# Attention of six heads on one Trainium2 core: products with V in four column groups instead of three, in twelve lots per image instead of sixteen

## Chip, cores and metric

The kernel runs on one core of one Trainium2 chip. The metric is the device time of one execution in microseconds. PE is TensorE, DVE is VectorE, ACT is ScalarE, POOL is GpSimd, SP is the engine that issues the DMAs.

## What is computed

The input is 32 images of 192 channels and 32 x 32 pixels, that is 1024 tokens of 192 numbers. Each image goes through three parts, each with a residual sum:

```python
x = x + proj(channel_attention(x))                  # 8 heads over channels, l2-normed
t = tokens(x)                                       # [B, 1024, 192]
z = ln(t); q, k, v = z @ Wq, z @ Wk, z @ Wv         # 6 heads of 32
att = softmax(causal(q @ k.T / sqrt(192)))
t = t + att @ v                                     # the part that is changed
t = t + ffn(ln(t))                                  # sign weights, absmax over groups of images
```

The causal attention is the large part: for each of 6 heads and each of 8 query tiles of 128 tokens, a query tile qt (0 to 7) sees the key tiles 0 to qt, so qt + 1 tiles.

## The kernel before, in words

**Groups and images.** 32 images are worked in five groups of six and a rest of two (`groups`, L343). A group is one long `attention` (PE L659, ACT L914, DVE L1202) over its six images, and then a tail (`group_tail`) with the feed-forward part of the six.

**Units and slots.** A unit is one head and one query tile; an image has UNITS = 48 of them (L48). The order of all the work is written out by hand in slots, one slot per unit, and each engine goes through the same slots in the same order. In slot n:

- PE makes the scores of unit n in PSUM (`S`, L672), adds the causal mask (L674), and turns (transposes) the probabilities of unit n - 3 (AHEAD, L53) into one or two banks `PT` of up to four tiles each (L686);
- DVE takes the row maximum of the scores of unit n (L1206) and copies the first bank of unit n - 3 from PT to SBUF (L378, called from `pt_copy`);
- ACT makes exp of unit n (L929) and copies the second bank of unit n - 3, if its qt is over 3 (L933, `by_act`).

The two halves of `S` alternate, so PE's scores of unit n + 2 wait for exp of unit n. The two banks PT alternate too, so a turn waits until the bank before last was copied. Small units (qt 0 to 3) are the even ones and large units (qt 4 to 7) the odd ones (TILES, L52).

**Products with V.** P times V needs the turned probabilities as the moving operand, 128 columns of f32, and 32 columns of V (one head) as weights. A lot of them (before: a triple, `triple_of`, L72) takes three units of the same query tile and of heads 3*grp to 3*grp + 2. Head number hh of a triple goes to PE's column group 32*hh and to rows 32*hh of the PSUM bank `OUT`, with `tile_position=(0, 32*hh)` (L706 to L708). The loop is over key tiles j outside and heads inside; I call one j of a lot a step. A triple of query tile qt has qt + 1 steps, each of three products, each of which is two matmul instructions. Triples run at slots 8 (small) and 11 (large) after the start of their block of six slots (PV_AT, L54), after the turns of that slot. An image has KI = 16 triples.

**Going back.** Four triples (BATCH, L55) fill the four places of 128 columns in `OUT`. ACT copies OUT to `oT` (L921, at slot OT_AT), PE turns oT into a PT bank (L715, at BACK_AT), and DVE (`add_to_t1`) multiplies by the reciprocals of the row sums and adds to `T1` (L1192, L1194, L1200). NBI = 4 such batches per image.

**Buffers of turned probabilities.** `PTS` is in `work`: a ring of four places for small units (4 x 512 columns) and of four for large ones (4 x 1024). `pt_copy` waits until the triple that last read the place has been multiplied (`pv_made`).

**Front work.** Beside the attention of image u, the channel attention, the layer norm and the projections of image u + 1 run in slots that SLOTS (L153) and SMALL_SLOTS (L158) fix: xt0 to xt3, g0, g1, wg0, wg1, na, rb, u, mt, t0 to t3, then z0 to z3, qk0 to qk5 and v0 to v3. On the way from "rb" (slot 15) to "u" (slot 18) lie the small channel softmax on DVE (logits, slot 16, L1109 to L1116), ACT (xexp, slot 17, L857) and DVE (attn, slot 17.5, L1119 and L1122). Layer norm statistics and normalisation are on DVE at slots 22, 25, 27, 28 and 29. After qk5, SP sends q and k with 16 DMAs per image to QS and KS (`front` of SP, L412 to L417), eight for heads 0 to 2 and then eight for heads 3 to 5; PE waits for the second eight at slot 24 (L663 to L665), and DVE at slot 9 (wg0, L1092). The slots of the front work are not touched by the change.

Of the kernel before, what the change touches and what calls it, by code (L numbers as in the profile page):

```python
# [18 lines left out]
F32 = mybir.dt.float32  # L19
# [40 lines left out]
RING = 4  # L60
STACKS = 8 * 16
# [5 lines left out]

def qtile(n):
    return TILES[n // 6 % 4][n % 2]


def triple_of(n):  # L72
    return 2 * (n // 6) + n % 2


def unit_of(k, hh):
    return 6 * (k // 2) + k % 2 + 2 * hh


def last_slot(images):  # L80
    return 12 * (NBI * images - 1) + BACK_AT


def triples_at(images, slot):

    return [k for k in range(KI * images) if 6 * (k // 2) + PV_AT[k % 2] == slot]


def batches_at(images, slot, at):

    return [j for j in range(NBI * images) if 12 * j + at == slot]

# [9 lines left out]


def sum_col(n):

    k = triple_of(n)
    return 3 * (BATCH * (k // BATCH % SUMS) + place(k)) + n % 6 // 2

# [13 lines left out]
CHUNKS = {images: transposed(images) for images in (2, GROUP)}  # L122
PT_IMG = len(CHUNKS[2]) // 4
assert all(len(c) == 2 * PT_IMG * images for images, c in CHUNKS.items())

# [36 lines left out]
def hybrid_kernel(nc, x, wa, wb, wv, wpt, bp, temp, w3, w1, b1, w2, b2, out):  # L162
# [5 lines left out]
    with ctx:  # L168
# [3 lines left out]
        def sem(name):  # L172
# [37 lines left out]
        NK = sb("NK", [CH, 4])  # L210
        RD = sb("RD", [CH, 2, CH])
        ATT = RD
        MT = sb("MT", [CH + 1, 2, C])
# [3 lines left out]
        PROD = hi_z[0:CH + 1, :].bitcast(F32)[:, 0:4 * C].rearrange("p (a b) -> p a b", a=2)  # L217
        T0 = sb("T0", [P, 2, TT, C])
# [14 lines left out]
        T1H = T1[:, :, :, :].rearrange("p b (h t) c -> p b h (t c)", h=2)  # L233
        work = sb("work", [P, 9216])

        PS = [work[:, 0:1024].rearrange("p (a b) -> p a b", a=2), work[:, 1024:3072].rearrange("p (a b) -> p a b", a=2)]
        PTS = [work[:, 3072:5120].rearrange("p (a b) -> p a b", a=RING),
               work[:, 5120:9216].rearrange("p (a b) -> p a b", a=RING)]

# [3 lines left out]
        OT = work[:, 4096:4096 + 4 * 4 * C].rearrange("p (s n) -> p s n", s=4)  # L243
        oT = sb("oT", [CH, BATCH * P])
        rowsum = sb("rowsum", [P, 3 * BATCH * SUMS])
# [4 lines left out]
        rsums = sb("rsums", [P, 3 * BATCH])  # L250
        gm1 = sb("gm1", [P, GS, MH])
# [119 lines left out]
        def pt_copy(eng, copy, g, images, i):  # L371

            _, _, m, c0, k = CHUNKS[images][i]
            eng.wait_ge(pt_full[i % 2], after(g, 0, PT_IMG, i // 2 + 1))
# [167 lines left out]
        def _(pe):  # L542
# [111 lines left out]
            for name in SLOTS:  # L654
                if name == "qk0":
                    pe.wait_ge(w3_ready, 1)
                front_part(name, 0, 0)

            def attention(g, images, fronts):  # L659
                for n in range(last_slot(images) + 1):  # L660
                    if n < UNITS * images:
                        u, h, qt = n // UNITS, 3 * (n % UNITS // 24) + n % 6 // 2, qtile(n)
# [13 lines left out]
                    for i, (_, kind, m, c0, k) in chunks_at(images, n):  # L676
                        bank = PT[i % 2]
# [3 lines left out]
                        if kind == "p":  # L681
                            if i >= 2:

                                pe.wait_ge(pt_free[i % 2], after(g, 0, PT_IMG, i // 2))
# [4 lines left out]
                    for k in triples_at(images, n):  # L689
                        u, grp, qt = k // KI, k % KI // 8, qtile(unit_of(k, 0))  # L690
                        done = [i for i, c in enumerate(CHUNKS[images]) if c[1] == "p" and c[2] <= unit_of(k, 2)]
                        for b in range(2):

                            pe.wait_ge(pt_free[b], after(g, 0, PT_IMG, max(i for i in done if i % 2 == b) // 2 + 1))
                        if k % KI == 0:

                            for step in STEPS[-2:]:
                                wait_freed(pe, g, u, step)
                        if k and k % BATCH == 0:

                            pe.wait_ge(oT_made, after(g, 0, NBI, k // BATCH))
                        o = P * place(k)
                        for j in range(qt + 1):
                            for hh in range(3):
                                h = 3 * grp + hh
                                last = mm(OUT[32 * hh:32 * hh + 32, o:o + P],  # L706
                                          V[u % 2][:, j, D * h:D * h + D], PTS[k % 2][:, unit_of(k, hh) // 2 % RING, P * j:P * j + P],
                                          start=(j == 0), stop=(j == qt), tile_position=(0, 32 * hh))  # L708
                        last.then_inc(pv_made, 1)
                    for i, (_, kind, j, _, _) in chunks_at(images, n):  # L710
                        if kind == "o":
                            pe.wait_ge(pt_free[i % 2], after(g, 0, PT_IMG, i // 2))
# [126 lines left out]
        def _(act):  # L839
# [74 lines left out]
            def attention(g, images, fronts):  # L914
                for n in range(last_slot(images) + 1):
                    for j in batches_at(images, n, OT_AT):
                        act.wait_ge(pv_made, after(g, 0, KI, BATCH * (j + 1)))
                        if j >= 1:

                            act.wait_ge(t1_step, after(g, 0, 3 * NBI, 3 * (j - 1) + 2))  # L920
                        A(oT[:, :], OUT[0:CH, :], ACT.Copy).then_inc(oT_made, 1)  # L921
                    if n < UNITS * images:

                        act.wait_ge(max_made, after(g, 0, UNITS, n + 1))
                        if n >= 4:
                            i = max(i for i, c in enumerate(CHUNKS[images]) if c[1] == "p" and c[2] == n - 4)
                            act.wait_ge(pt_full[i % 2], after(g, 0, PT_IMG, i // 2 + 1))
                        w = P * (qtile(n) + 1)
# [69 lines left out]
        def _(dve):  # L998
# [185 lines left out]
            def add_to_t1(g, i, j):  # L1184

                base = after(g, 0, 3 * NBI, 3 * j)
                dve.wait_ge(pt_full[i % 2], after(g, 0, PT_IMG, i // 2 + 1))
                n = 3 * BATCH
                u, grp, qts = j // NBI, j % NBI // 2, batch_tiles(j)
# [4 lines left out]
                v.tensor_tensor(t1.rearrange("p t (h d) -> p t h d", h=3),  # L1194
                                PT[i % 2][:, 0:BATCH * CH].rearrange("p (t h d) -> p t h d", t=BATCH, h=3),
                                rsums[:, :].rearrange("p (t h) -> p t h", t=BATCH).unsqueeze(3).broadcast_to(
                                    [P, BATCH, 3, D]), ALU.mult).then_inc(t1_step, 1)
                dve.wait_ge(t1_step, base + 2)
# [185 lines left out]
```

## Time and profile before

| | us |
|---|---|
| median of 3 runs | 4620.59 (4613.62 to 4620.93) |
| profiled execution, its own time | 4622.14 |
| span of the profile | 4620.3 |
| PE busy | 4051.6 (88%) |
| DVE busy | 3328.1 (72%) |
| ACT busy | 2688.6 (58%) |
| mean granted TensorE clock | 0.976 |

The profiled execution is 1.5 us above the median and its span 1.8 us below its own time. PE is the busiest engine, but a busy share is a mean over stages: within an image, stretches of slots differ, which the section of rows takes one by one. Inside a group, images that nothing disturbs last 105.5 us each. The stretches in which one image is read below are its slots 0 to 10, 11 to 18, 19 to 23, 24 to 31 and 32 to 47, and then the whole image.

### The profile page before, as it was taken

To read this page: it belongs to the slowest core of one execution; us is meant where nothing else is said; L and a number is where in the kernel's file an instruction comes from. 1 tells how busy PE (TensorE), PEld (TensorE's weight loads), DVE (VectorE), ACT (ScalarE), POOL (GpSimd) and SP (SyncE) were. 2 spreads that over 40 slices of the span, in tenths; PEclk is the share of its full clock that TensorE was granted. 3 is DMA by queue.
4 is the path that set the end of the run, shared out by engine and by line. 5 is a ranking of instruction groups with operands and counts; after the bars stand their busy time and mean duration, and the time that the engine had idled before them with its cause. 6 is when DMAs were issued, how large, how long until landed. Compare 5 with 4: busy or idle time off the path is not lost.

```text
span 4620.3 us, 114708 instructions
## 1 busy us (share of the span) xinstructions
PE 4051.6 (88%) x39240; PEld 2942.2 (64%) x39240; DVE 3328.1 (72%) x6327; ACT 2688.6 (58%) x5901; POOL 363.2 (8%) x374
## 2 busy tenths in 40 slices
PE   6989988979999888999888879999888999888888
PEld 4667665566766646667665666666646666665665
DVE  5777776767777767777776767777767777776776
ACT  2555556556656655565566556665655555556555
POOL 1000002000000110000002000000110000002000
PEclk7999999999999999999999999999999999999999
DMA  2111111011221101111111011211101111111011
GB/s 71 36 36 36 43 36 28 0 49 36 49 50 36 36 0 42 36 36 36 42 36 28 0 49 42 55 39 36 36 0 42 36 36 42 36 36 28 0 42 42
DMA packets 48635, 160.95 MB, mean 35 GB/s; under 512 B 12420, under 2 KB 12934, under 8 KB 48006
## 3 DMA queue, kind: packets, MB, share of 16 engines
q1 hardware_dynamic: 48134, 154.39, 14.0%
q8 instruction: 300, 4.92, 0.5%
q14 instruction: 201, 1.65, 0.1%
HBM read 28.52 MB, written 25.17 MB: 12 GB/s over the span
## 4 chain that ended last, share of the span: by engine, by line
PE 61%; DVE 16%; issue 15%; ACT 4%; POOL 2%; DVEq 1%; DMA 1%; ACTq 0%; SPq 0%; POOLq 0%
PE PT L686 10%; PE OUT L706 10%; PE S L672 5%; PE PT L804 5%; PE S L731 4%; DVE nmax L1206 4%; DVE work L378 4%; PE S L630 2%; PE FR L630 2%; PE S L775 2%; PE FR L574 2%; DVE XT L1077 2%; PE FR L637 1%; PE S L637 1%; PE S L674 1%
## 5 line engine op out<-in xcount | busy, mean ns | idle before, releaser
L929 ACT ACTIVATE work<-S,nmax 128x256 f32<-128x256 f32 (+7 forms) x1536 | 1137.2, 741 | 1115.0 <-DVE nmax L1206 1056.0
L1206 DVE TENSOR_REDUCE nmax<-S 128x1 f32<-128x256 f32 (+7 forms) x1536 | 1156.0, 753 | 780.2 <-PE S L674 760.4
L686 PE MATMUL PT<-ident,work 128*128 128x128 f32 x6912 | 1111.5, 281 | 224.8 <-DVE work L378 195.6
L686 PEld LDWEIGHTS PT<-ident,work 128*128 128x128 f32 x6912 | 746.7, 142 | 441.4 <-DVE work L378 259.4
L378 DVE COPY work<-PT 128x512 f32<-128x512 f32 (+3 forms) x1536 | 892.8, 581 | 41.4 <-PE PT L686 35.3
L672 PE MATMUL S<-KS,QS 128*128 128x512 f16 (+3 forms) x1152 | 323.6, 336 | 62.2 <-ACT work L929 29.0
L674 PE MATMUL S<-causal,identb 128*128 128x128 bf16 x1536 | 339.4, 221 | 0.0
L672 PE MATMUL S<-odd 128*128 128x512 f16 (+3 forms) x1152 | 314.8, 328 | 22.9 <-ACT work L929 21.5
L933 ACT ACTIVATE work<-PT 128x512 f32<-128x512 f32 (+3 forms) x768 | 330.6, 430 | 3.5 <-PE PT L686 3.4
L1240 DVE TENSOR_REDUCE gm<-S 128x1024 f32 (+1 forms) x180 | 220.0, 1222 | 119.4 <-PE S L775 119.1
L706 PE MATMUL OUT<-work,odd 128*32 128x128 f32 x6912 | 304.9, 277 | 0.0
L706 PE MATMUL OUT<-work,V 128*32 128x128 f32 x6912 | 303.5, 276 | 0.0
L731 PE MATMUL S<-odd,W1b 128*128 (+1 forms) x1080 | 258.5, 392 | 49.8 <-ACT work L972 41.5
L929 ACT ACTIVATION_READ_ACCUMULATOR work<-S,nmax 128x1 f32 x1536 | 300.9, 196 | 0.0
L775 PE MATMUL S<-odd,W1b 128*128 (+1 forms) x1080 | 293.4, 381 | 0.0
L972 ACT ACTIVATE work<-S,sc 128x512 f32<-128x512 f32 x360 | 254.6, 782 | 51.1 <-PE S L731 50.7
L706 PEld LDWEIGHTS OUT<-work,odd 128*32 128x32 f32 x6912 | 236.6, 110 | 39.6 <-issue 31.0
L706 PEld LDWEIGHTS OUT<-work,V 128*32 128x32 f32 x6912 | 234.4, 110 | 40.4 <-issue 32.7
L804 PE MATMUL PT<-W2b,work 128*128 128x192 f16 x2880 | 247.5, 246 | 8.8 <-DVE odd L1293 8.8
L804 PEld LDWEIGHTS PT<-W2b,work 128*128 128x128 f16 x2880 | 238.8, 98 | 23.4 <-DVE odd L1293 9.9
L1285 DVE SCALAR_TENSOR_TENSOR work<-work 128x1024 f16<-128x1024 f32 x180 | 218.3, 1225 | 29.6 <-ACT work L979 25.4
L674 PEld LDWEIGHTS S<-causal,identb 128*128 128x128 bf16 x1536 | 151.5, 99 | 123.9 <-issue 10.8
(207 smaller groups left out, 5952.6 us busy)
## 6 DMA issues: line engine op xcount, KB each, us to landing
X<-in_x SPq DMA_DIRECT2D x32, 768.0 KB, 5.3
odd<-hi_z SPq DMA_DIRECT2D x128, 192.0 KB, 4.2
odd<-odd SPq DMA_DIRECT2D x128, 192.0 KB, 4.2
out_y<-work SPq DMA_DIRECT2D x64, 384.0 KB, 3.8
QS<-hi_z SPq DMA_DIRECT2D x64, 192.0 KB, 4.0
QS<-odd SPq DMA_DIRECT2D x64, 192.0 KB, 4.0
KS<-hi_z SPq DMA_DIRECT2D x64, 192.0 KB, 4.3
KS<-odd SPq DMA_DIRECT2D x64, 192.0 KB, 4.6
```

Of the source, the lines that this page charges most:

```text
L378: copy(PTS[m % 2][:, m // 2 % RING, P * c0:P * (c0 + k)], PT[i % 2][:, 0:P * k]).then_inc(pt_free[i % 2], 1)
L672: mm(S[:, n % 2, c0:min(w, c0 + 512)], q, KS[u % 2][:, h, c0:min(w, c0 + 512)], start=True, stop=c0 + 512 < w)
L674: mm(S[:, n % 2, w - P:w], identb[:, :], causal[:, :], start=False, stop=True).then_inc(scores_full, 1)
L686: last = tr(bank[:, P * (j - c0):P * (j - c0) + P], PS[m % 2][:, m // 2 % 2, P * j:P * j + P], ident[:, :])
L706: last = mm(OUT[32 * hh:32 * hh + 32, o:o + P], V[u % 2][:, j, D * h:D * h + D], PTS[k % 2][:, unit_of(k, hh) // 2 % RING, P * j:P * j + P ...
L731: last = mm(bank, W1b[:, j, P * (i % 6):P * (i % 6) + P], rhs[:, j, :], start=(j == 0), stop=(j == 2))
L775: last = mm(bank, W1b[:, j, P * m:P * m + P], Z2[:, b, hf, j, :], start=False, stop=(j == 2))
L804: last = mm(PT[tp % 2][:, C * t:C * t + C], HS[:, hf, part, m, o:o + P], W2b[:, m, :], start=(m == 0 and part == 0), stop=(m == MH - 1 and ...
L929: A(PS[n % 2][:, n // 2 % 2, 0:w], S[:, n % 2, 0:w], ACT.Exp, bias=nmax[:, n % MAXES:n % MAXES + 1], accum_out=rowsum[:, sum_col(n):sum_co ...
L933: pt_copy(act, lambda o, x: A(o, x, ACT.Copy), g, images, i)
L972: A(H[:, i % MH, :], Y[i % 4], ACT.Gelu, bias=rb1[:, i % MH:i % MH + 1], scale=r1).then_inc(gelu_made, 1)
L1206: v.tensor_reduce(nmax[:, n % MAXES:n % MAXES + 1], S[:, n % 2, 0:P * (qtile(n) + 1)], AX.X, ALU.max, negate=True).then_inc(max_made, 1)
```

## The change

It renames the lots from triples to quads and changes six things.

1. A quad has four units, hh = 0 to 3, in column groups 0, 32, 64 and 96, and fills all 128 rows of OUT. Blocks have eight slots. Blocks 0 to 3 of an image hold heads 0 to 3 with one small and one large query tile each, (1, 7), (3, 5), (0, 6), (2, 4). Blocks 4 and 5 hold heads 4 and 5 with two small and two large query tiles: (0, 1) and (6, 7), then (2, 3) and (4, 5). There are KI = 12 quads per image, with a step for each key tile of the larger unit, and the shorter unit leaves its column group idle in the last step.
2. Large quads are multiplied at slot 12 after the start of their block and small ones at slot 15, so large before small. The function `times_v` is called after the scores and before the turns of its slot; before, the products came after the turns.
3. oT, its copy, the turning back (128 rows by 128 columns instead of 96) and add_to_t1 work on four heads of four query tiles, or on two heads of eight, NBI = 3 times per image; OT_AT, BACK_AT go from 18, 19 to 24, 25.
4. Small turned probabilities lie at places of their real widths, in a buffer of 2304 columns that even and odd blocks fill from its two ends (`turned_at`). Large ones stay in four places of 1024.
5. PE waits for the q and k of the second three heads at slot 6 of an image, where head 3 comes first, instead of at slot 24.
6. RD and MT of the channel attention move into the memory of hi_z, behind PROD.

```diff
 UNITS = NH * TT
-KI = UNITS // 3
+KI = UNITS // 4
 GROUP = 6

 TILES = [(1, 7), (3, 5), (0, 6), (2, 4)]
+PAIRS = [((0, 1), (6, 7)), ((2, 3), (4, 5))]
 AHEAD = 3
-PV_AT = (8, 11)
+PV_AT = (15, 12)
 BATCH = 4
 NBI = KI // BATCH
...
-OT_AT, BACK_AT = 18, 19
-RING = 4
+OT_AT, BACK_AT = 24, 25
+SMALL = 2304
...
+def head_and_tile(n):
+
+    block, at, large = n % UNITS // 8, n % 8 // 2, n % 2
+    if block < 4:
+        return at, TILES[block][large]
+    return 4 + at % 2, PAIRS[block - 4][large][at // 2]
+
+
 def qtile(n):
-    return TILES[n // 6 % 4][n % 2]
+    return head_and_tile(n)[1]
...
+def lots_until(k):
+
+    return k if k % 2 else k + 2
 
 def unit_of(k, hh):
-    return 6 * (k // 2) + k % 2 + 2 * hh
+    return 8 * (k // 2) + k % 2 + 2 * hh
...
+def turned_at(m):
+
+    k, hh = quad_of(m), m % 8 // 2
+    if m % 2:
+        return 1024 * hh
+    widths = [P * (qtile(unit_of(k, i)) + 1) for i in range(hh + 1)]
+    return SMALL - sum(widths) if k // 2 % 2 else sum(widths[:hh])
+
+def overwritten(m):
+
+    k = quad_of(m)
+    return k - 2 if m % 2 or m % 8 >= 4 else k - 4
...
-            if m >= 2 * RING:
-
-                eng.wait_ge(pv_made, after(g, 0, KI, triple_of(m - 2 * RING) + 1))
-            copy(PTS[m % 2][:, m // 2 % RING, P * c0:P * (c0 + k)], PT[i % 2][:, 0:P * k]).then_inc(pt_free[i % 2], 1)
+            if overwritten(m) >= 0:
+
+                eng.wait_ge(pv_made, after(g, 0, KI, lots_until(overwritten(m))))
+            at = turned_at(m) + P * c0
+            copy(PTS[m % 2][:, at:at + P * k], PT[i % 2][:, 0:P * k]).then_inc(pt_free[i % 2], 1)
...
+            def times_v(g, images, k):
+                u, units = k // KI, [unit_of(k, hh) for hh in range(4)]
+                done = [i for i, c in enumerate(CHUNKS[images]) if c[1] == "p" and c[2] <= units[3]]
+                for b in range(2):
+
+                    pe.wait_ge(pt_free[b], g * PT_GROUP + (max(i for i in done if i % 2 == b) // 2 + 1))
...
+                if k > BATCH and k % BATCH == 1:
+
+                    pe.wait_ge(oT_made, after(g, 0, NBI, k // BATCH))
+                o = P * place(k)
+                for j in range(max(qtile(m) for m in units) + 1):
+                    for hh, m in enumerate(units):
+                        h, qt = head_and_tile(m)
+                        if j <= qt:
+                            last = mm(OUT[32 * hh:32 * hh + 32, o:o + P], V[u % 2][:, j, D * h:D * h + D],
+                                      PTS[k % 2][:, turned_at(m) + P * j:turned_at(m) + P * j + P],
+                                      start=(j == 0), stop=(j == qt), tile_position=(0, 32 * hh))
+                last.then_inc(pv_made, 1)
...
-                        if n % 24 == 0:
-
-                            pe.wait_ge(stacked[n % UNITS // 24], after(g, u, STACKS, STACKS))
+                        if n % UNITS in (0, 6):
+
+                            pe.wait_ge(stacked[h // 3], after(g, u, STACKS, STACKS))
...
+                    for k in quads_at(images, n):
+                        times_v(g, images, k)
                     for i, (_, kind, m, c0, k) in chunks_at(images, n):
...
-                                last = tr(PT[i % 2][:, CH * q:CH * q + CH], oT[:, P * q:P * q + P],
-                                          ident[0:CH, 0:CH])
+                                last = tr(PT[i % 2][:, P * q:P * q + P], oT[:, P * q:P * q + P], ident[:, :])
...
-                        A(oT[:, :], OUT[0:CH, :], ACT.Copy).then_inc(oT_made, 1)
+                        A(oT[:, :], OUT[:, :], ACT.Copy).then_inc(oT_made, 1)
...
-                ts, cols = slice(qts[0], qts[-1] + 1, 2), slice(CH * grp, CH * grp + CH)
+                if j % NBI < 2:
+                    ts, cols, nt, nh = slice(qts[0], qts[-1] + 1, 2), slice(0, 4 * D), 4, 4
+                else:
+                    ts, cols, nt, nh = slice(0, TT), slice(4 * D, C), TT, 2
```

The lines of the old loop over triples, taken out of `attention` on PE, are L689 to L709 above. Semaphore counts follow the new numbers of lots and banks.

## Rows read from the trace of the kernel before

**Rows 1.** The page, parts 1 and 4: busy time of PE, and the chain by engine.

```profile
PE 4051.6 (88%) x39240; PEld 2942.2 (64%) x39240; DVE 3328.1 (72%) x6327; ACT 2688.6 (58%) x5901; POOL 363.2 (8%) x374
...
PE 61%; DVE 16%; issue 15%; ACT 4%; POOL 2%; DVEq 1%; DMA 1%; ACTq 0%; SPq 0%; POOLq 0%
```

**Rows 2.** Stretches of one image: us, then busy PE, PEld, DVE, ACT, POOL; then PEclk.

```profile
1168.60:1191.70 23.10, 21.87 (x204) 16.78 (x202) 16.11 (x26) 14.15 (x36) 0.00 (x0) 1.00 0.16 37
1191.70:1209.90 18.20, 15.03 (x196) 11.93 (x195) 11.90 (x28) 8.53 (x25) 1.00 (x1) 1.00 0.01 2
1209.90:1223.20 13.30, 13.07 (x126) 11.31 (x125) 9.17 (x24) 7.03 (x19) 0.00 (x0) 1.00 0.01 2
1223.20:1238.80 15.60, 11.41 (x115) 7.48 (x114) 14.85 (x35) 9.07 (x21) 5.02 (x4) 1.00 0.20 51
1238.80:1274.10 35.30, 34.48 (x391) 25.07 (x389) 25.92 (x44) 24.37 (x57) 0.00 (x0) 1.00 0.31 68
1168.60:1274.10 105.50, 95.86 (x1023) 72.58 (x1021) 77.94 (x155) 63.16 (x155) 6.02 (x5) 1.00 0.17 39
```

**Rows 3.** Who made PE wait: total us, times, longest us.

```profile
PE PT L686 <- DVE work L378: 195.6, 442, 1.0
```

**Rows 4.** Timeline of PE, slot 11: start us, duration us, what, count.

```profile
1192.09 0.61 PE L686 MATMUL PT<-ident,work 128*128 128x128 f32 x4
1192.63 1.95 PE L706 MATMUL OUT<-work,V 128*32 128x128 f32 x48
1194.51 1.52 PE L591 MATMUL FR<-ones,hi_z 97*96 97x1 f32 x16
```

**Rows 5.** Timeline of PE, slots 17 to 20; idle before it and releaser in brackets.

```profile
1204.88 0.28 PE L686 MATMUL PT<-ident,work 128*128 128x128 f32 x1
1205.09 1.51 PE L706 MATMUL OUT<-work,V 128*32 128x128 f32 x36
1206.53 0.34 PE L672 MATMUL S<-KS,QS 128*128 128x384 f16 x1
...
1209.14 0.89 PE L606 MATMUL FR<-WPT,RD 96*96 96x192 f32 x4 [1.45 <-DVE RD L1122]
...
1213.54 0.42 PE L706 MATMUL OUT<-work,V 128*32 128x128 f32 x6
```

**Rows 6.** Groups by form: copy to oT, turning back, and adding back; busy us, mean ns.

```profile
L1194 DVE TENSOR_TENSOR T<-PT,rsums 128x384 f32<-128x384 f32 x128 | 71.3, 557 | 4.4
...
L921 ACT ACTIVATE oT<-OUT 96x512 f32<-96x512 f32 x128 | 74.2, 580 | 9.8 <-PE OUT L706 9.8
...
L715 PE MATMUL PT<-ident,oT 96*128 96x96 f32 x512 | 69.3, 259 | 24.3 <-ACT work L933 19.1 <-ACT oT L921 4.7
```

**Rows 7.** Groups by form: DVE's maxima and first-bank copies.

```profile
L1206 DVE TENSOR_REDUCE nmax<-S 128x1 f32<-128x1024 f32 x192 | 234.2, 1220 | 81.4 <-PE S L674 81.4
...
L1206 DVE TENSOR_REDUCE nmax<-S 128x1 f32<-128x128 f32 x192 | 55.2, 288 | 190.7 <-PE S L674 174.7 <-DVE odd L1141 15.7
...
L378 DVE COPY work<-PT 128x512 f32<-128x512 f32 x960 | 654.3, 682 | 35.4 <-PE PT L686 29.4
...
L378 DVE COPY work<-PT 128x128 f32<-128x128 f32 x192 | 53.7, 280 | 0.0
```

**Rows 8.** Timeline of DVE, slot 15: the maximum behind slot 14's lot.

```profile
1202.16 1.09 DVE L1206 TENSOR_REDUCE nmax<-S 128x1 f32<-128x896 f32 x1 [0.94 <-PE S L674]
```

**Rows 9.** SP's last q and k DMAs of an image, and median us to landing.

```profile
1168.25 1.52 SPq L416 DMA_DIRECT2D KS<-odd  x2
...
KS<-odd SPq DMA_DIRECT2D x64, 192.0 KB, 4.6
```

**Rows 10.** Busy time and clock (PEclk) of whole images: undisturbed, and two with falls.

```profile
406.50:512.00 105.50, 95.85 (x1022) 72.57 (x1019) 77.92 (x155) 63.16 (x155) 6.02 (x5) 1.00 0.17 39
512.00:622.20 110.20, 100.44 (x1023) 76.26 (x1021) 78.20 (x155) 63.60 (x155) 6.03 (x5) 0.95 0.16 37
2031.10:2138.00 106.90, 97.16 (x1023) 73.94 (x1019) 77.94 (x155) 63.44 (x155) 6.03 (x5) 0.98 0.17 39
```

More of the change, by code:

```diff
@@ L65, with quad_of, quads_at @@
          284: "next_stats1", 285: "next_aggregate", 286: "turn0", 287: "turn1", 288: "turn2", 289: "turn3"}
-def qtile(n):
-    return TILES[n // 6 % 4][n % 2]
-def triple_of(n):
-    return 2 * (n // 6) + n % 2
+def head_and_tile(n):
[3 more added lines that the diff above has]
+    return 4 + at % 2, PAIRS[block - 4][large][at // 2]
+def qtile(n):
+    return head_and_tile(n)[1]
+def quad_of(n):
+    return 2 * (n // 8) + n % 2
+def lots_until(k):
+    return k if k % 2 else k + 2
 def unit_of(k, hh):
-    return 6 * (k // 2) + k % 2 + 2 * hh
+    return 8 * (k // 2) + k % 2 + 2 * hh
 def last_slot(images):
-    return 12 * (NBI * images - 1) + BACK_AT
-def triples_at(images, slot):
-    return [k for k in range(KI * images) if 6 * (k // 2) + PV_AT[k % 2] == slot]
+    return 16 * (NBI * images - 1) + BACK_AT
+def quads_at(images, slot):
+    return [k for k in range(KI * images) if 8 * (k // 2) + PV_AT[k % 2] == slot]
 def batches_at(images, slot, at):
-    return [j for j in range(NBI * images) if 12 * j + at == slot]
+    return [j for j in range(NBI * images) if 16 * j + at == slot]
 def batch_tiles(j):
@@ L101, in place @@
     return batch_tiles(k // BATCH).index(qtile(unit_of(k, 0)))
+def turned_at(m):
[7 more added lines that the diff above has]
+    return k - 2 if m % 2 or m % 8 >= 4 else k - 4
 def sum_col(n):
-    k = triple_of(n)
-    return 3 * (BATCH * (k // BATCH % SUMS) + place(k)) + n % 6 // 2
+    k = quad_of(n)
+    return 4 * (BATCH * (k // BATCH % SUMS) + place(k)) + n % 8 // 2
 def transposed(images):
@@ L122 @@
 CHUNKS = {images: transposed(images) for images in (2, GROUP)}
-PT_IMG = len(CHUNKS[2]) // 4
-assert all(len(c) == 2 * PT_IMG * images for images, c in CHUNKS.items())
+PT_GROUP = len(CHUNKS[GROUP]) // 2
+assert len(CHUNKS[GROUP]) == 2 * PT_GROUP
 STEPS = ["xt0", "xt1", "xt2", "xt3", "g0", "g1", "wg0", "wg1", "na", "rb", "u", "mt", "t0", "t1", "t2", "t3",
@@ L216, in hybrid_kernel @@
         zcat = hi_z[:, :].rearrange("p (a b) -> p a b", a=TT)
-        PROD = hi_z[0:CH + 1, :].bitcast(F32)[:, 0:4 * C].rearrange("p (a b) -> p a b", a=2)
+        mix = hi_z[0:CH + 1, :].bitcast(F32)
+        PROD = mix[:, 0:4 * C].rearrange("p (a b) -> p a b", a=2)
+        RD = mix[0:CH, 4 * C:5 * C].rearrange("p (a b) -> p a b", a=2)
+        ATT = RD
+        MT = mix[:, 5 * C:7 * C].rearrange("p (a b) -> p a b", a=2)
         T0 = sb("T0", [P, 2, TT, C])
@@ L657, in _ @@
                 front_part(name, 0, 0)
+            def times_v(g, images, k):
[3 more added lines that the diff above has]
+                    pe.wait_ge(pt_free[b], g * PT_GROUP + (max(i for i in done if i % 2 == b) // 2 + 1))
+                if k % KI == 1:
+                    for step in STEPS[-2:]:
+                        wait_freed(pe, g, u, step)
+                if k > BATCH and k % BATCH == 1:
[9 more added lines that the diff above has]
+                last.then_inc(pv_made, 1)
             def attention(g, images, fronts):
@@ L682, in attention @@
                             if i >= 2:
-                                pe.wait_ge(pt_free[i % 2], after(g, 0, PT_IMG, i // 2))
+                                pe.wait_ge(pt_free[i % 2], g * PT_GROUP + i // 2)
                             for j in range(c0, c0 + k):
@@ L688, in attention @@
                             last.then_inc(pt_full[i % 2], 1)
[L689 to L709, printed above, removed]
                     for i, (_, kind, j, _, _) in chunks_at(images, n):
                         if kind == "o":
-                            pe.wait_ge(pt_free[i % 2], after(g, 0, PT_IMG, i // 2))
+                            pe.wait_ge(pt_free[i % 2], g * PT_GROUP + i // 2)
                             pe.wait_ge(oT_made, after(g, 0, NBI, j + 1))
                             for q in range(BATCH):
-                                last = tr(PT[i % 2][:, CH * q:CH * q + CH], oT[:, P * q:P * q + P],
-                                          ident[0:CH, 0:CH])
+                                last = tr(PT[i % 2][:, P * q:P * q + P], oT[:, P * q:P * q + P], ident[:, :])
                             last.then_inc(pt_full[i % 2], 1)
@@ L926, in attention @@
                             i = max(i for i, c in enumerate(CHUNKS[images]) if c[1] == "p" and c[2] == n - 4)
-                            act.wait_ge(pt_full[i % 2], after(g, 0, PT_IMG, i // 2 + 1))
+                            act.wait_ge(pt_full[i % 2], g * PT_GROUP + (i // 2 + 1))
                         w = P * (qtile(n) + 1)
```

32 lines of the change are left out of this document (14 added, 18 removed).

## The prediction

> **What bounds the kernel now.** I read the page first, then the windows by stretch of one image, then who made PE wait, and last the timeline of PE around the products. The page says that PE is busy 88% and holds 61% of the chain, with DVE next at 16% [rows 1]. That is a mean. Within an image the five stretches differ [rows 2]. In slots 0 to 10, 19 to 23 and 32 to 47 PE is busy 21.87 of 23.1, 13.07 of 13.3 and 34.48 of 35.3 us: there PE's own work is the time. In slots 24 to 31 DVE is busy 14.85 of 15.6 us and PE 11.41: layer norm lies there beside the largest units, and DVE is the bound. In slots 11 to 18 neither is full (PE 15.03, DVE 11.90 of 18.2): a chain of short steps bounds it. Over the image PE idles 9.6 of 105.5 us. What it waits for is mostly DVE's copies out of PT [rows 3]. So work taken from PE counts in the first three stretches and little in the other two.
>
> **The price of a step of products.** The lot of 48 instructions (8 steps) lasts 1.95 us [rows 4], the lot of 6 instructions (1 step) 0.42 [rows 5]. The slope is (1.95 - 0.42) / 7 = 0.2186 us per step. A step has three products of two instructions each, and one turn, a single instruction, follows another at (0.61 - 0.28) / 3 = 0.11 us, from four of them against one [rows 4, 5]. So 0.2186 us is two instructions in a row, one column group's own share, and the three groups run wholly beside each other. A fourth group should cost nothing per step. By the Trainium skill, page "TensorE: Matmul & The Clock Gate", section "Why this matters for your kernels", packing is less than perfect: 2.38 times for three column tiles and 3.07 for four row tiles. That would make a step of four 4/3.07 against 3/2.38, or 3% dearer, an estimate of 0.4 us per image. The trace's three groups are at 3.0 times, so I take no surcharge.
>
> A lot also has a fixed cost. The last turn ahead of it starts at 1192.09 + 0.61 - 0.28 = 1192.42, the lot at 1192.63, which is 0.10 more than a turn's pace; it takes 1.88 us to the next start at 1194.51, against 8 x 0.2186 = 1.75 [rows 4]. That is 0.10 + 0.13 = 0.23 us per lot.
>
> **The change on PE.** Steps before: 2 groups of heads x 36 = 72 per image. After: 36 for heads 0 to 3, and 2 + 8 + 4 + 6 = 20 for heads 4 and 5, so 56. 16 x 0.2186 = 3.5 us per image. Four lots fewer: 4 x 0.23 = 0.9. Turning back goes from 16 x 96 to 12 x 128 columns, the same 1536, and loses one entry; the four instructions are 69.3 / 128 = 0.54 us at each of 4 times [rows 6], so I take 0.3 saved, with 0 and 0.5 as ends. Sum on PE: 4.7 us per image, 151 for 32 images. That is the most the products can give.
>
> **Where it falls.** Both orders, counted slot by slot (steps, lots before; after): slots 0-10: 10, 3; 10, 2. Slots 11-18: 18, 3; 10, 2. Slots 19-23: 8, 2; 10, 2. Slots 24-31: 8, 2; 8, 2. Slots 32-47: 28, 6; 18, 4.
> - Slots 0-10: one lot fewer, -0.23, but three more tiles are turned (53 to 56), +0.33. I take 0.
> - Slots 19-23: two steps more, +0.44; the turning back leaves, -0.4, and two tiles fewer are turned, -0.2. I take -0.2.
> - Slots 32-47: -10 x 0.2186 - 2 x 0.23 = -2.65, four tiles fewer turned, -0.4, four more scored, about +0.2. PE is 98% busy there. But slots 32 to 35 lose both their lots, and ACT's and DVE's parts stand in the open; I let 0.45 of the 2.85 go to that and take -2.4.
> - Slots 24-31, DVE's: it reduces 40 tiles before and 32 after. A tile more costs (1.220 - 0.288) / 7 = 0.133 us in the maximum and (0.682 - 0.280) / 3 = 0.134 in a copy [rows 7]. -8 x 0.133 + one copied tile 0.13 + 0.25 for a longer adding back = -0.7; I take -0.5. The lot of 7 steps at slot 28 is hidden beside the layer norm.
> - Slots 11-18: PE loses 8 steps and one lot, -2.0 us, and gets four more turned tiles. Yet this stretch ends with u, which waits 1.45 us for the channel softmax on DVE, directly behind the 6 steps of slot 17 [rows 5]. Those 1.51 us lay in the shadow of that softmax. Without them PE waits about 1.45 + 1.44 = 2.9 us. And DVE gets more ahead of u: first-bank copies of units 8 to 15 go from 26 to 32 tiles and maxima from 33 to 35, +1.0 us. In return slot 14's lot of four steps is gone, behind which DVE waited 0.94 us for its next maximum [rows 8]; I count -0.8. And at slot 12 the lot of 8 steps now stands before the turns, so DVE's copy waits until it is over, +0.2. I take +0.3.
>
> Sum: 0 - 0.2 - 2.4 - 0.5 + 0.3 = -2.8 us per image, -90 us over 32.
>
> **The other edits.** DVE loses one round of adding back per image: two operations of 384 columns at 0.557 [rows 6] four times is 4.5 us, three times at 512 is some 4.1 (128 columns more at 0.133 per 128), so -0.4, in the shadow of PE outside slots 24 to 31. The round now at slot 9 stands ahead of the product that "na" needs at slot 11; uncovered, it would cost up to 1 us. ACT loses one copy of 0.58 [rows 6], hidden. The wait for heads 3 to 5 moves from slot 24 to slot 6. The last pair of q and k DMAs is issued from 1168.25 on, for 1.52 us, and lands 4.6 us after issue, by 1174.4 [rows 9]; slot 6 begins at 1168.6 plus most of 12 us, so it is hidden with some 5 us to spare; without that cover PE would wait in front of the scores of slot 6, and DVE and ACT with it. The waits for places: a large unit's place is freed by the lot of the same slot, which PE now does before the turns, so the copy, queued behind the turn, never waits for more. RD and MT in hi_z come after PROD, whose wait for the stacks covers them: 0. The groups' drains are two slots longer without scores: a step or two of products each, 0 to +3 us in all; I take 0.
>
> **The clock.** In this trace five of 32 images are longer because the clock fell from full to half for a moment. The granted share over the image is 0.95 at 110.2 us and 0.98 at 106.9, against 1.00 at 105.5 [rows 10]. The falls come behind slots 18 and 30, where PE waits. Those waits get longer at slot 18. I add 10 us, some two such images; the ends are -13 (no falls) and +127 (27 more images with +4.7).
>
> Profiled execution: 4622.1 - 90 + 10 = 4542. It stands 1.5 us over the median shown, so the forecast is 4540.
>
> **Rivals.**
> - *All of it arrives.* If DVE and ACT keep ahead and the waits at slots 24 to 31 shrink with the lighter units, the full 4.7 us per image comes: 4620 - 151 = 4470. For it: 98% busy in the longest stretch. Against: 9.6 us of idle that other engines set. Chance 0.15.
> - *Waits eat it.* Products ahead of the turns starve DVE and ACT in each of six large lots, of which I counted one. If each costs 0.4 us more, 77 us over 32 images, about 4615 comes out. For it: DVE's copy is the main releaser of PE [rows 3]. Against: an engine that PE bounds has room. Chance 0.13.
> - *The fourth group runs after the other three* (slower). Its place is each step with four products, 52 of 56. If they take two rounds, it is +52 x 0.2186 = 11.4 us per image, and -2.8 becomes +8.6: 4620 + 275 = 4895. It decides as soon as a step costs over 0.2186 + 2.8 / 52 = 0.27 us. No row shows a fourth group, so it can't be excluded; three without any loss speak against it. Chance 0.04. The Trainium skill, same page, section "Step-by-step: what each phase is for", lists for the buses that feed the column groups that quadrant 3 "has a HW bug, not supported"; this would be that case.
> - *The clock falls in most images* (slower), as bounded above: 4540 + 117 = 4657, and it cancels the gain from about 18 more images at +4.7 on. Five images of 32 fall now. Chance 0.04.
>
> The likeliest case has 0.64. A measurement of this kernel can tell 0.2%, about 9 us. Faster: 0.64 + 0.15 and half of the 0.13, so 0.85; the same 0.06; slower 0.09. The range goes from just below the full gain to about where waits eat most of it: 4465 to 4605.
>
> **What would show it.** Lots of 64 instructions (8 steps, fewer in the last) that last 1.95 to 2.0 us confirm the price of a step; 2.5 or more refute it. Undisturbed images should last 102 to 103.5 us, slots 32 to 47 about 33, slots 11 to 18 still 18 to 19 with a wait of 2.5 to 3 us at u. PE's busy time per image falls from 95.9 to some 91. I am wrong if the stretches of slots 0 to 10 or 32 to 47 show new idle time of PE behind DVE or ACT, or if the clock falls in more than ten images.

## The result: 3.3% slower, and the profile after

The changed kernel takes 4773.3 us (median of 4 runs, 4763.7 to 4775.5) against 4617.1 for the kernel before in the same comparison. The ratio is 1.0332, with a 95% interval of 1.0317 to 1.0348. The forecast was 4540, with a range up to 4605. The span of the profiled execution is 4761.9 us, 141.6 over the one before.

The page of the changed kernel, parts 1 and 4, answers to [rows 1]:

```profile
PE 4056.4 (85%) x39112; PEld 2957.2 (62%) x39112; DVE 3355.8 (70%) x6231; ACT 2691.4 (57%) x5869; POOL 363.4 (8%) x374
...
PE 59%; DVE 16%; issue 14%; ACT 6%; POOL 2%; DVEq 1%; DMA 1%; SPq 1%; ACTq 0%; POOLq 0%
```

All three engines are busy for a smaller share, so what was added is mostly time that is not their work. The products did what was forecast. This is the timeline of PE at slot 12 of one image, with a lot of 64 instructions, eight steps of four products, and from slot 15 a lot of two steps.

```profile
1112.48 0.22 PE L727 MATMUL S<-causal,identb 128*128 128x128 bf16 x1
1112.63 1.96 PE L707 MATMUL OUT<-work,odd 128*32 128x128 f32 x64
1114.52 0.87 PE L741 MATMUL PT<-ident,work 128*128 128x128 f32 x6
...
1118.75 0.64 PE L707 MATMUL OUT<-work,odd 128*32 128x128 f32 x16
```

1.96 us, against 1.95 for eight steps of three [rows 4]. The lot of 16 instructions, two steps of four, takes 0.64, so a step of four costs (1.96 - 0.64) / 6 = 0.22 us. The fourth column group is free, and the rival in which it runs after the other three is out. The stretches of one image, in the order of [rows 2]:

```profile
1086.00:1108.90 22.90, 22.01 (x218) 17.20 (x216) 16.76 (x27) 14.90 (x36) 0.00 (x0) 1.00 0.20 46
1108.90:1127.80 18.90, 14.75 (x172) 10.97 (x171) 13.44 (x29) 9.59 (x28) 1.00 (x1) 0.98 0.01 2
1127.80:1141.70 13.90, 13.90 (x151) 11.98 (x150) 7.83 (x20) 6.82 (x16) 0.00 (x0) 0.91 0.01 2
1141.70:1159.00 17.30, 11.19 (x131) 8.26 (x129) 15.56 (x37) 7.95 (x21) 5.03 (x4) 0.96 0.19 46
1159.00:1195.20 36.20, 33.03 (x354) 23.96 (x353) 25.26 (x41) 24.12 (x55) 0.00 (x0) 0.97 0.27 59
1086.00:1195.20 109.20, 94.89 (x1018) 72.37 (x1016) 78.84 (x152) 63.39 (x154) 6.03 (x5) 0.97 0.16 37
```

The image lasts 109.2 us, not 105.5. Two things are to be seen. The clock column is under 1.00 in four stretches, in an image that is as ordinary as the one of [rows 2]: in the clock's record the granted clock falls to half at least twice in each of the first 31 images, for 3.4 us or more each time: once 39 to 42 us after the image's start (at slot 18), and again 64 to 76 us after it (behind slots 27 to 31). The last image, beside which no front work runs, has no fall. Inside images it is 87 falls with 364 us at half, against 8 with 37 us before. And PE idles 14.3 us of the image (109.20 - 94.89) instead of 9.6. The timeline of PE in slots 17 and 18, up to the first scores of slot 19, has the first of both, to be read against [rows 5]:

```profile
1121.76 0.66 PE L741 MATMUL PT<-ident,work 128*128 128x128 f32 x4
1122.25 0.22 PE L725 MATMUL S<-odd 128*128 128x128 f16 x1
1122.31 0.22 PE L727 MATMUL S<-causal,identb 128*128 128x128 bf16 x1
1122.36 0.61 PE L741 MATMUL PT<-ident,work 128*128 128x128 f32 x4
1124.69 0.44 PE L741 MATMUL PT<-ident,work 128*128 128x128 f32 x2 [1.72 <-DVE work L408]
1126.61 1.38 PE L636 MATMUL FR<-WPT,hi_z 96*96 96x192 f32 x4 [1.48 <-DVE hi_z L1155]
```

The lot of six steps that stood here is gone, and in slot 18 PE stands still for 1.72 us for a copy by DVE and 1.48 us for the channel softmax, together 3.2 us instead of 1.45. Right behind it the four products of u take 1.38 us instead of 0.89: they run, for the most part, at half clock.

### The profile page after: what moved, and what is told of

The parts are those of the page before. It is cut to its first block, busy times and chain, and to the rows that moved or that the text cites. A ratio compares the mean times of both kernels' runs of the same rounds, so it can differ in the third digit from the quotient of the medians.

```text
span 4761.9 us, 113993 instructions
## 1 busy us (share of the span) xinstructions
PE 4056.4 (85%) x39112; PEld 2957.2 (62%) x39112; DVE 3355.8 (70%) x6231; ACT 2691.4 (57%) x5869; POOL 363.4 (8%) x374
## 4 chain that ended last, share of the span: by engine, by line
PE 59%; DVE 16%; issue 14%; ACT 6%; POOL 2%; DVEq 1%; DMA 1%; SPq 1%; ACTq 0%; POOLq 0%
PE PT L741 10%; PE OUT L707 9%; PE S L725 5%; PE PT L837 5%; DVE nmax L1242 5%; PE S L764 4%; DVE work L408 3%; PE FR L660 2%; PE S L660 2%; PE S L808 2%; PE FR L604 2%; PE S L641 2%; ACT work L962 2%; PE S L667 1%; PE S L727 1%
## 5 line engine op out<-in xcount | busy, mean ns | idle before, releaser
L741 PE MATMUL PT<-ident,work 128*128 128x128 f32 x6912 | 1153.8, 289 | 310.4 <-DVE work L408 247.0
L741 PEld LDWEIGHTS PT<-ident,work 128*128 128x128 f32 x6912 | 769.2, 146 | 557.0 <-DVE work L408 307.8
L725 PE MATMUL S<-KS,QS 128*128 128x512 f16 (+3 forms) x1152 | 334.8, 346 | 52.5 <-issue 22.6
L725 PE MATMUL S<-odd 128*128 128x512 f16 (+3 forms) x1152 | 324.8, 337 | 14.2 <-ACT work L962 11.9
L707 PE MATMUL OUT<-work,V 128*32 128x128 f32 x6912 | 254.3, 290 | 0.4
L707 PE MATMUL OUT<-work,odd 128*32 128x128 f32 x6912 | 241.8, 281 | 3.1 <-ACT work L966 3.1
L707 PEld LDWEIGHTS OUT<-work,V 128*32 128x32 f32 x6912 | 198.4, 116 | 42.8 <-issue 30.6
L707 PEld LDWEIGHTS OUT<-work,odd 128*32 128x32 f32 x6912 | 190.7, 113 | 42.0 <-issue 31.4
```

The lines of the kernel that those rows point to most:

```text
L707: last = mm(OUT[32 * hh:32 * hh + 32, o:o + P], V[u % 2][:, j, D * h:D * h + D], PTS[k % 2][:, turned_at(m) + P * j:turned_at(m) + P * j + P],
```

## The experiments

The experiments ran in three sets, each beside the kernel before (4616.4, 4616.8 and 4618.6 us). The changed kernel itself was measured once, in the comparison above. Gains against it are differences of medians from different sets; worked out from the ratios to the kernel before, they are up to 6 us smaller.

**Fillers: is it the clock?** Into the changed kernel I put fillers where PE waits: turns of the identity whose results nobody reads.

```diff
                 elif name == "u":
+                    for _ in range(24):
+                        tr(FR[:, 384:512], ident[:, :], ident[:, :])
                     pe.wait_ge(xsoft, after(g, u, XSOFT, XSOFT))
```

> The changed kernel, with 24 turns of the identity into unused columns of FR put before the wait at u (slot 18); nothing else differs. They take about 24 x 0.11 = 2.6 us of a wait of 3.2 us and compute nothing that is used. Theory A (the clock falls because PE stands still at u): the fall about 41 us after the start of each image is gone, the one about 71 us stays, an image lasts some 107.5 instead of 109.2 us, and the kernel some 4700 to 4725. Theory B (only waits for DVE and ACT cost the time, the clock is a by-product): the fillers take the place of idle time, and the time stays at 4762 to 4775.

Measured: 4738.6 us (4734.1 to 4741.2). The fall at 41 us is gone from every image, which refutes theory B. But the gain is 35 us, not 50 to 75. Falls behind slots 27 to 31 remain, and six images now have one at 26 to 28 us, where four had one without the fillers. In all it is 65 falls with 248 us at half. Without the falls at slot 18, the changed kernel had 56 with some 211 us. So when one fall was taken away, others moved or got longer.

The second run adds 18 and 12 fillers ahead of the turns of slots 27 and 30:

```diff
+FILL = {27: 18, 30: 12}
...
+                    if n % UNITS in FILL and n // UNITS < fronts:
+                        wait_freed(pe, g, n // UNITS + 1, "t2")
+                        for _ in range(FILL[n % UNITS]):
+                            tr(FR[:, 384:512], ident[:, :], ident[:, :])
```

> The changed kernel, with the 24 turns before u and also 18 turns of the identity in slot 27 and 12 in slot 30, where PE waits for DVE's copies beside the layer norm (2.4 and 1.6 us of idle). Theory A: no falls of the clock inside images, an image lasts 105 to 106.5 us, the kernel 4620 to 4670, that is at or slightly over the kernel before, since the waits remain. Theory B: 4762 or more, as the fillers stand in the way of the turns.

Measured: 4670.1 us (4662.5 to 4677.4), 103 us faster than the changed kernel with 54 more turns per image, at the upper edge of theory A. Falls: 12, with 48 us at half, where none was expected; five of them are in the last image of a group. The stretches of one image show the changed order at full clock:

```profile
1065.70:1088.30 22.60, 21.97 (x216) 17.19 (x217) 16.72 (x27) 14.61 (x36) 0.00 (x0) 1.00 0.20 46
1088.30:1107.70 19.40, 16.74 (x196) 13.35 (x195) 13.47 (x29) 9.62 (x28) 1.00 (x1) 1.00 0.01 1
1107.70:1120.60 12.90, 12.87 (x151) 11.19 (x150) 7.83 (x20) 6.82 (x16) 0.00 (x0) 1.00 0.01 3
1120.60:1137.30 16.70, 13.87 (x161) 10.89 (x159) 15.28 (x37) 7.32 (x21) 5.03 (x4) 1.00 0.17 48
1137.30:1172.60 35.30, 32.24 (x355) 23.02 (x353) 25.43 (x41) 24.44 (x55) 0.00 (x0) 1.00 0.27 60
```

Two thirds of the loss (103 of 156 us) came back with the clock. The rest is in these rows: even at full clock this image lasts 106.9 us (others 106.7 to 107.7; the fillers at u add some 0.5), longer than 105.5. And yet PE has less real work: in an image of e9 below, without a fall or fillers, it is busy for 92.22 us, 3.6 less than before. Slots 11 to 18 and 24 to 31 got 1.2 and 1.1 us longer, and slots 32 to 47 gained nothing.

**Less work ahead of the wait, in the kernel before.** This asks the same from the other side. Of the lot directly ahead of u, five of the six steps are left out, so the kernel's results lack those products.

```diff
-                        for j in range(qt + 1):
+                        last_j = 0 if n % UNITS == 17 else qt
+                        for j in range(last_j + 1):
...
-                                          start=(j == 0), stop=(j == qt), tile_position=(0, 32 * hh))
+                                          start=(j == 0), stop=(j == last_j), tile_position=(0, 32 * hh))
```

> The kernel before, with only the first key tile of the products at slot 17 of each image (one step of three products instead of six); the other five steps of that lot are left out of the computation, so each image has 1.09 us less work on PE, directly ahead of the wait at u. Theory A: the wait at u grows from 1.45 to about 2.5 us, the clock now falls behind it in most images instead of three, and the kernel is 20 to 80 us slower than 4617 with less work. Theory B: the wait grows by what the work shrank, the clock stays, and the time is the same within 5 us, or up to 35 us lower.

Measured: 4661.9 us (4659.7 to 4662.4), ratio 1.0099, interval 1.0082 to 1.0116: 45 us slower with 1.09 us less work per image. PE's idle time in slot 18 went from 1.45 to 2.33 us, and 30 of the first 31 images have a fall behind slot 18, where before 3 had one. The timeline of PE in slot 18:

```profile
1110.33 0.55 PE L686 MATMUL PT<-ident,work 128*128 128x128 f32 x3 [0.55 <-DVE work L378]
1112.66 0.91 PE L606 MATMUL FR<-WPT,RD 96*96 96x192 f32 x4 [1.78 <-DVE RD L1123]
```

And the windows of three whole images, with no fall, with one of 3.4 us, and with one of 6.8 us; the clock is the third number from the right:

```profile
3691.70:3797.20 105.50, 94.96 (x993) 71.42 (x991) 77.93 (x155) 63.16 (x155) 6.03 (x5) 1.00 0.17 39
1287.00:1393.80 106.80, 96.50 (x993) 72.57 (x990) 78.08 (x155) 63.17 (x155) 6.02 (x5) 0.98 0.17 39
1178.80:1287.00 108.20, 97.90 (x992) 73.74 (x989) 78.09 (x155) 63.27 (x155) 6.02 (x5) 0.97 0.16 38
```

The first row is the point of this case. It is the one image of the 31 without a fall, and it still lasts 105.50 us: the 1.09 us of work were worth nothing, since they lay in the cover of the softmax chain, that is, PE did them while it had to wait for that chain anyway. With a fall an image is 1.3 or 2.7 us longer. This is 0.4 us for each us at half clock. By the same price the 327 more us at half in the changed kernel are an estimated 130 us, of which the fillers of e2 gave back 103 net of their own cost.

**The order within a slot.** The call of `times_v` moves behind the turns, one slot earlier:

```diff
-PV_AT = (15, 12)
+PV_AT = (14, 11)
...
-                    for k in quads_at(images, n):
-                        times_v(g, images, k)
                     for i, (_, kind, m, c0, k) in chunks_at(images, n):
...
                             last.then_inc(pt_full[i % 2], 1)
+                    for k in quads_at(images, n):
+                        times_v(g, images, k)
```

> The changed kernel, with the products with V again behind the turns of their slot, one slot earlier (PV_AT = (14, 11)). If the products ahead of the turns starve DVE and ACT (theory C): DVE's wait for PT falls from 331 us to under 60, as before, and the kernel gets 30 to 80 us faster. If the order within the slot does not matter (A or B alone): within 10 us of 4773, with two falls of the clock per image as now.

Measured: 4767.1 us (4765.3 to 4776.3), so theory C is out as a cause of the time, at least for the order that the kernel before had. From the list of DVE's waits (us in total, times, longest):

```profile
DVE nmax L1242 <- PE S L727: 788.6, 740, 8.7
...
DVE work L408 <- PE PT L739: 29.0, 87, 0.8
```

The wait of DVE's copies for PT fell from 331 to 29 us, as C expected; but DVE's wait for scores rose from 571 to 789 us. So most of it is DVE waiting for the same lots, only in front of another instruction. The two orders are close to each other: a lot after the turns of slot 11 also stands ahead of the turns of slot 12.

**The two waits, each by itself.** First the chain of the channel softmax, one slot earlier:

```diff
-         "na": 11, "rb": 15, "u": 18, "mt": 19, "t0": 20, "t1": 21, "t2": 22, "t3": 23, "z0": 31, "z1": 32,
+         "na": 11, "rb": 14, "u": 18, "mt": 19, "t0": 20, "t1": 21, "t2": 22, "t3": 23, "z0": 31, "z1": 32,
...
-SMALL_SLOTS = {"norms": 12, "rdiag": 13, "logits": 16, "xexp": 17, "attn": 17.5, "ln_stats0": 22, "ln_stats1": 25,
+SMALL_SLOTS = {"norms": 12, "rdiag": 13, "logits": 15, "xexp": 16, "attn": 17, "ln_stats0": 22, "ln_stats1": 25,
```

> The changed kernel, with rb one slot earlier (14), logits at 15, xexp at 16 and attn at 17, u still at 18: the chain of the channel softmax starts one slot earlier and nothing else differs. If the wait at u is what lets the clock fall behind slot 18 and what makes slots 11 to 18 long (theory A with the lost cover): the wait falls from 3.2 to under 1.5 us, slots 11 to 18 from 18.9 to about 17.5, the fall at 41 us is gone in most images, the kernel 4690 to 4720. If the stretch is bound by DVE's own work there (theory D): the wait moves to the turns of slots 12 to 16, stretch and falls stay, within 10 us of 4773.

Measured: 4676.8 us (4668.4 to 4680.0), 96 us faster, which is more than expected. Slots 11 to 18 fell from 18.9 to 17.2 us, slot 18's wait from 3.2 to 0.5, with 1.3 us coming back at the turns of slot 17. Falls: 56, with 201 us at half, and only one image has one at 41 us. So the gain is both the shorter wait and the clock.

Then the turning and adding back of an image's first batch, from slot 25 to slot 31:

```diff
-        out += [(slot, "o", j, 0, 0) for j in batches_at(images, slot, BACK_AT)]
+        out += [(slot, "o", j, 0, 0) for j in range(NBI * images) if 16 * j + (31 if j % NBI == 0 else BACK_AT) == slot]
```

> The changed kernel, with the turning and adding back of the first batch of each image at slot 31 instead of 25, behind the layer norm instead of in front of its statistics. If the 1.6 us of adding back on DVE at slot 25 are what made slots 24 to 31 longer than before (theory E): PE's idle time there falls from 6.2 to about 4.8 us, the stretch from 17.3 to about 16, the kernel 30 to 50 us faster. If DVE's sum over the stretch decides (it stays the same with slot 31 in it): within 10 us of 4773.

Measured: 4691.8 us (4681.4 to 4701.8), 81 us faster. PE's idle time in slots 24 to 31 fell from 6.2 to about 4.4 us and the stretch from 17.3 to 15.9 us; that is 1.4 x 32 = 45 us, within what theory E gave (30 to 50). The whole gain is over it. For the rest the clock is the likely reason, though no run isolates it: 71 falls with 272 us at half, against 364, is an estimated 37 us at 0.4 us each.

Both together, and both with small fillers (`range(8)` at u, `FILL = {27: 12, 30: 8}`):

> Both of the last two edits. Theories A and E: their gains add, 4640 to 4690. If the falls of the clock only move to another idle stretch, less than the sum.

> Both edits and small fillers: 8 turns of the identity before u, 12 in slot 27 and 8 in slot 30. They compute nothing that is used. Theory A: no falls inside images, an image lasts 104.5 to 106 us and the kernel 4590 to 4630. If waits alone decide, as the run without fillers or up to 20 us slower.

Measured: 4606.0 us (4602.6 to 4610.7), ratio to the kernel before 0.9976 (0.9966 to 0.9985), and 4604.1 us, ratio 0.9975 (0.9965 to 0.9985). Both moves gained 167 us, nearly the sum of 96 and 81, and more than e7's text expected. The fillers took the falls from 42 to 20 and gave nothing that can be told from the spread: leaving out the first and the last image of each group, those without a fall last 104.6 to 104.8 us, and those of e7 with one fall of 3.4 us behind slot 30 or 31 last 104.2 to 105.3. In slots 11 to 18 the 8 fillers at u cost 0.4 us, as there is hardly a wait left.

**The cover ahead of qk0.** The timeline of PE in the changed kernel has this wait at slot 35:

```profile
1164.31 0.28 PE L741 MATMUL PT<-ident,work 128*128 128x128 f32 x1
1165.78 0.39 PE L660 MATMUL FR<-zt,W3h 128*128 128x512 f16 x1 [1.19 <-ACT zt L915]
```

Before, a lot of 2 steps at slot 32 and one of 8 steps at slot 35 stood ahead of it. So I put the lot of 5 steps from slot 36 to 35, on top of both moves:

```diff
-    return [k for k in range(KI * images) if 8 * (k // 2) + PV_AT[k % 2] == slot]
+    return [k for k in range(KI * images) if 8 * (k // 2) + PV_AT[k % 2] - (k % KI == 7) == slot]
```

> The changed kernel with both moves (chain one slot earlier, first adding back at slot 31), and in addition the large lot of block 3 (5 steps) at slot 35 instead of 36, so in front of qk0. If qk0's wait of 1.2 us for ACT's copy of zt is open because the lots that stood at slots 32 and 35 before have left (theory F, lost cover): the wait at slot 35 falls to about 0.1, slots 32 to 47 get 1.0 us shorter, and the kernel 20 to 35 us faster than with both moves alone (4606), about 4575 to 4585. If ACT's own sum of work over slots 31 to 35 decides: the wait moves to slots 36 to 38 and the time stays within 5 us.

Measured: 4594.0 us (4589.2 to 4594.3), ratio 0.9942 (0.9929 to 0.9956), 12 us faster than e7 (16 by the two ratios), less than the 20 to 35 of theory F. The wait at slot 35 fell from 1.2 to 0.6 or 0.7 us: the lot itself now waits there, for ACT's copy of the second bank. So part of that wait was lost cover and part is ACT's own work. This is the one image of e9, first and last of each group aside, without a fall:

```profile
2986.40:3090.10 103.70, 92.22 (x1017) 69.95 (x1016) 78.60 (x153) 63.08 (x154) 6.02 (x5) 1.00 0.17 38
```

The same with `FILL = {27: 12, 30: 8}` and none at u:

> The kernel of e9 with fillers, 12 turns of the identity in slot 27 and 8 in slot 30. Theory A: falls behind slot 27 to 31 vanish, which with both moves cost about 1.2 us per image; the fillers themselves cost up to 0.5; so 0 to 20 us faster than e9.

Measured: 4579.2 us (4574.5 to 4587.3), ratio 0.9914 (0.9900 to 0.9928), the fastest of all, with 25 falls instead of 48. Here the fillers of slots 27 and 30 paid, with 15 us. One of its images, whole, by the windows:

```profile
1260.20:1363.60 103.40, 94.35 (x1035) 72.05 (x1036) 78.56 (x152) 62.92 (x154) 6.03 (x5) 1.00 0.17 40
```

**The same remedies for the kernel before.** The first is the diff of the chain, one slot earlier, in the kernel before:

> The kernel before, with the same chain one slot earlier (rb 14, logits 15, xexp 16, attn 17), so that the changed kernel's gain from it can be told from what any order gains. If the lot of 6 steps at slot 17 covered most of the chain: the wait at u goes from 1.45 to 0 and is partly back as waits of slots 14 to 17; stretch 11 to 18 falls by 0.3 to 1.2 us, the kernel by 10 to 40 us. If it was only slack: the same within 5 us.

The second has, in the kernel before, `for _ in range(10): tr(FR[:, 384:512], ident[:, :], ident[:, :])` ahead of the wait at u:

> The kernel before with 10 turns of the identity before u (1.1 us of the 1.45 us of waiting). Theory A: the falls behind slot 18 in images 4, 24 and 28 are gone, some 8 us of 4617. The fillers may delay u by 0.1 us each time. So 0 to 10 us faster; slower than 4620 would speak against fillers as a remedy.

Measured: 4612.5 us, ratio 0.9988 (0.9979 to 0.9997), and 4610.2 us, ratio 0.9982 (0.9973 to 0.9991). With the chain earlier, undisturbed images went from 105.5 to 104.7 us, but there are 19 falls instead of 8 (106.2 us with one), which ate most of it. 17 of them are in slot 17, although PE now waits less in slots 11 to 18 (2.7 us instead of 3.2 in all, the longest wait 0.7 instead of 1.45). So a longer wait in front of u brings falls (e4), but the length of the waits alone doesn't say where they come. With 10 fillers at u only 3 falls were left. So the earlier chain is worth 6 us to the old order and 96 us to the new one. The best new order is 18 us under the old one with the earlier chain (4594.0 against 4612.5), and with fillers 31 us under the old one with fillers (4579.2 against 4610.2). This isn't a fair price of the four column groups: the old order got one remedy at a time, neither a later adding back nor the earlier chain together with fillers, so how far it would go with as much tuning was not tested.

## Why the prediction was wrong

**The price of the products was right.** A step of four costs what a step of three does, 56 steps instead of 72, and no surcharge showed at eight steps (1.96 against 1.95 us). The Trainium skill, "TensorE: Matmul & The Clock Gate", section "Step-by-step: what each phase is for", lists quadrant 3 of the buses as "not supported"; no such thing shows here in f32 products with a tile position. The sum on PE was high: forecast 4.7 us less per image, measured 3.6 at full clock (92.22 against 95.86 us busy).

**Two steps failed, of about the same size: the term for the clock, and the sum of the stretches at full clock.** The clock was priced at +10 us, and the fillers alone gave back 103. The stretches were priced at -2.8 us per image, -90 us in all, and gave no gain but a loss: 53 us remain in e2, of which the fillers at u are an estimated 15.

**The clock.** I added 10 us, with +127 as the far end and a chance of 0.04. I had written that the falls come behind slots 18 and 30, that PE waits there, and that the wait at slot 18 would double, and then priced that as two more images. The runs show 87 falls instead of 8. Experiment e4 is the missing link: 0.9 us more of waiting takes the images with a fall at slot 18 from 3 to 30 of 31. In the kernel before, three images had that fall already, and it took little to bring it to nearly all. The number of falls was too low too, since an image now has two or three, where I had counted images.

**Slots 32 to 47: forecast -2.4 us, measured about 0** at full clock (35.3 us in the image of e2 above, about 35.4 in most others, 35.3 in [rows 2]). PE's work did fall, to 32.2 us from 34.5, and the idle time rose from 0.8 to 3.1. I had let 0.45 us go to "ACT's and DVE's parts in the open". It was 2.3. The waits are now 1.2 us ahead of qk0, 0.85 ahead of v1, where the bank is freed late by DVE, and the rest at the turns of slots 34 and 46. "PE is 98% busy there" was true only because the lots stood where the other engines were late.

**Slots 24 to 31: forecast -0.5, measured +1.1 at full clock** (16.7 us in e2). The term that failed is "0.25 for a longer adding back". The timelines of DVE have this for the multiplication of the adding back, in the kernel before (slot 31) and in the changed one (slot 25):

```profile
1238.89 0.56 DVE L1194 TENSOR_TENSOR T<-PT,rsums 128x384 f32<-128x384 f32 x1
...
1144.93 0.69 DVE L1230 TENSOR_TENSOR T<-PT,rsums 128x512 f32<-128x512 f32 x1
```

Before, DVE came to it only at 1238.89, when the stretch was over (1238.80 in [rows 2]); now it lies in the middle, directly in front of the statistics of the layer norm. So the stretch got a whole adding back, three operations of 0.25, 0.69 and 0.69 us, and not 0.25 us more. DVE's work in it was to fall by 0.7 us and rose by 0.7, from 14.85 to 15.56. In e6, with the adding back at slot 31, DVE does it behind the stretch again (2246.68, the stretch ends at 2246.6), and the stretch is 1.4 us shorter.

**Slots 11 to 18: forecast +0.3, measured +0.7** (18.9 us, the last 0.9 of them at half clock), by the mechanism as described: a wait at slot 18 of 2.9 us forecast, 3.2 measured (1.72 of it for DVE's copy ahead of u). Slots 0 to 10 (forecast 0, measured -0.2) and 19 to 23 (forecast -0.2, measured -0.4 in e2 at full clock) were about right.

**The ends of the groups: forecast 0 to +3 us in all.** In e2 the 26 images that have another of their group behind them take 41 us more in all than before. The last images of the five groups, each with the tail behind it, take 15 us more in all, with five falls among them. In e7, e8, e9 and e11, where the former are 20 to 44 us shorter than before, the latter are still 6 to 10 us longer. No run was made to find out why.

So at full clock the sum was about +1.4 us per image (106.9 against 105.5, with some 0.5 of it the fillers') instead of -2.8. Two of the signs that I had named for being wrong came: new idle time of PE in slots 32 to 47, and a fall in more than ten images. The rival "waits eat it" came true in its effect and not in its reason: I had it from the lots ahead of the turns, and putting them behind the turns changed nothing (e3). What mattered was what the lots had covered: moving the chain, the adding back and one lot each brought time back. Why the falls that are left stand where they do in one image and not in the next was not settled: e1 shows that taking one away moves others, and e10 that they can come with shorter waits.

## What to carry to other kernels

A stretch in which the busiest engine is 98% busy can be bound by the others as soon as some of that work is taken out: look at what ends the waits then, slot by slot, and not at the sum of the stretch. And look at when an engine really does the work of a slot: DVE did slot 31's when PE was in slot 32, and so it stood in another sum. When a change takes PE's work from in front of a wait, count that work as worth nothing, and ask what the clock does, above all where some repetitions of the same loop already show a fall. Such places are cheap to test with fillers in front of the wait. And an order that was good around one grouping of products has to be set again around another: here three small moves turned 3.3% slower into 0.6% faster, and fillers into 0.9%.

## What the runs showed of the hardware

Leaving out 1.09 us of work per image made a kernel 45 us slower. The granted clock accounts for it: at its lower level (1.2 instead of 2.4 GHz) for 3.4 us it costs an image 1.3 us, and for 6.8 us 2.7 us, while the one image without a fall lasted as long as before. And work of no use, 54 turns in each image, made a kernel 103 us faster. Four column groups run f32 products beside each other as three do, at 0.22 us per step. The fixed cost of a lot is also the same. Behind a turn in f32 it starts 0.21 us after it [rows 4], 0.10 more than a turn's pace of 0.11. Behind the mask's bf16 product it starts 0.15 us after it (1112.48 to 1112.63), again 0.10 more than the 0.05 in which a turn follows that product (1122.31 to 1122.36).
